# A graph network on one core: a smaller descriptor scratch, and a longer ring of gathered rows

## The chip, the core and the metric

The kernel runs on one core of one Trainium2 chip. The metric is device microseconds of one execution: the kernel before took 3387.86 us (median of 3 runs, 3387.04 to 3388.99).

## The reference, cut to what matters

A graph of 3125 nodes with 128 features and 50000 edges, sorted by destination, goes through a two-layer graph convolution (its input rows are all the same row, so it needs no gather), and then through five attention layers with two heads. The attention layers take most of the time. One of them, in the reference's words:

```python
edge_emb = edge_attr_full @ ew.T + eb
xw = x @ W
xj = xw[src].reshape(-1, H, D) + edge_emb.reshape(-1, H, D)
xi = xw[dst].reshape(-1, H, D)
alpha = einsum('ehd,hd->eh', xi, att_i) + einsum('ehd,hd->eh', xj, att_j)
alpha = leaky_relu(alpha, 0.2)
ea = exp(alpha - segment_max(alpha, dst)[dst])
alpha = ea / (segment_sum(ea, dst)[dst] + 1e-16)
out = segment_sum(xj * alpha[..., None], dst).mean(axis=1) + b
```

Each edge needs the row of its source node (`src` is random), and each node is also its own neighbour, by 3125 added self edges that carry no attributes.

## The kernel before, in words

**Tiles, groups and chunks.** The edges are cut into 391 tiles of 128. Four tiles make a group (98 groups), and 28 tiles make a chunk: chunks 0 to 12 have 28 tiles, chunk 13 has 16, chunk 14 has 11 (`CH`, `TC`, `GROUPS`, lines 45 to 51). Every layer goes once over all of them.

**The gathers.** At the start of a layer SP writes the node table (a row is 128 features and two scores) to memory in five pieces. When these have landed, POOL issues 391 indirect DMAs, one a tile: each fetches 128 rows of 520 bytes by the indices in `srci` into one slot of `ring`, a buffer of `RING` = 60 slots (lines 502 to 513). Tile t goes to slot (t + 25) % `RING` (line 68): the first 25 slots hold the nodes' own rows `xt` at the start of a layer, so the first gathers go behind them. Three waits hold a gather back:

```python
if t == RING - SHIFT:
    pool.wait_ge(aj_read, layer + 1)
if RING - SHIFT <= t < RING - SHIFT + NT:
    pool.wait_ge(tr_ps, NT * layer + t - (RING - SHIFT) + 1)
if t >= RING and (t == RING or GROUP_OF[t - RING] != GROUP_OF[t - RING - 1]):
    pool.wait_ge(sums, layer * G + GROUP_OF[t - RING] + 1)
```

The first two (from tile 35 on with 60 slots) wait until `xt` has been read by VectorE (line 1208) and transposed by TensorE (line 758). The third, from tile 60 on, waits until TensorE has summed the group that last lay in the slot. A gather raises one of five semaphores `gath`, by its chunk's number modulo five, when it has landed.

**A chunk's way through the engines.** ScalarE copies, for each tile, a window of 24 destination scores (`windows`, line 580). VectorE reduces these windows (`windows_sum`, lines 1087 to 1096). Then `chain_scan` (lines 1099 to 1123) waits until all gathers of the chunk have landed, adds the sources' scores out of `ring` (line 1105, and line 1108 in addition where the chunk's slots wrap past the end of the ring), and starts a running maximum. `chain_rows` and `chain_cols` (lines 1125 to 1156) end it, ScalarE takes the exponential (line 586), and `chain_probs` (line 1166) writes the weights and makes the first two groups' one-hot weights with `weigh` (line 1161).

**Sums.** For each group TensorE clears a bank (line 741), and for each of its tiles multiplies the ring's rows by the weights (line 745) and the edges' attributes by the one-hots (line 747); the last of them raises `sums`. VectorE adds the bank into `acc` (`add_group`, line 1200). In chunks 0 to 8 up to three tiles of a second product, `self_tile` (line 783), go between a chunk's groups.

**The order of the work** is written out by hand in each engine's program. On VectorE the chain of chunk c+1 is laid into the groups of chunk c: the windows' sums behind its first three groups, `chain_scan` behind the add of its third group, rows and columns behind the fourth, `chain_probs` behind the sixth (`chain_at`, line 89). `weigh` runs four groups ahead of `add_group`. In chunk 13 the places are the first, second and third group.

**The end of a layer.** When all groups are added, 25 node tiles are multiplied, scaled, added and written back to `xt`, and the next layer's table is written.

**The scratch.** The descriptors of the gathers are generated on the chip into a reserved stretch at the front of each partition of SBUF, by default 16 KB long (`dynamic_dma_scratch_size` of the constructor at line 1368).

Of the kernel before, what the change touches and what calls it, by code (L numbers as in the profile page):

```python
# [48 lines left out]
G = len(GROUPS)  # L49
GC = [[g for g in range(G) if GROUPS[g][0] == c] for c in range(NC)]  # L50
GROUP_OF = [g for g in range(G) for _ in range(GROUPS[g][2])]
RING = 60
SHIFT = 25
NGATH = 5
NAT = 3
# [7 lines left out]
POOL_MUL = (1, 3, 5)  # L63
assert TC[NC] == REAL and RING >= SHIFT + NT


def slot(t):
    return (t + SHIFT) % RING

# [28 lines left out]
def program(nc, x, src_rows, src_key, src_flat, dst_col, dst_next_col, dst_flat, dst_first,  # L98
            attr, W1, b1, W2, b2,
            weights, weightsT, attT, edge_w, edge_b, edge_woT, biases, edge_bias, out):  # L100
    with ExitStack() as ctx:
        def sb(name, shape, dt=F32):
            return ctx.enter_context(nc.sbuf_tensor(name, shape, dt))
# [13 lines left out]
        ai_rows = sb("ai_rows", [P, H, NP])  # L117
        ring = sb("ring", [P, RING, ROW])
        onehot = sb("onehot", [P, TILES, WIN])
# [67 lines left out]
        def part(base, n, dt=F32):  # L187
            words = n if dt != BF16 else (n + 1) // 2
            v = base[:, cut[0]:cut[0] + words]
            cut[0] += words  # L190
            return v if dt == F32 else v.bitcast(dt)[:, 0:n]
# [43 lines left out]
        s_parts = part(rowsf, 3 * NT, BF16).rearrange("p (q h) -> p q h", q=3)  # L235
        assert cut[0] <= RING * ROW
        cut[0] = NT * ROW
# [229 lines left out]
        def _(pool):  # L467
# [32 lines left out]
            for layer in range(LAYERS):  # L500
                pool.wait_ge(table_w, 16 * (len(TABLE_CUTS) - 1) * (layer + 1))
                for t in range(REAL):
# [4 lines that stand above are left out]
# [871 lines left out]
```

## Time and profile before

| what | value |
|---|---|
| time, median of 3 runs | 3387.86 us (3387.04 to 3388.99) |
| the profiled execution, first to last instruction | 3764.7 us |
| before the first gather | 475.5 us |
| a layer's gathers, first to last issue (layers 1 to 5) | 565.7, 567.9, 568.6, 566.0, 566.6 us |
| from a layer's last gather to the next layer's first (after layers 1 and 2) | 92.0, 89.1 us |
| busy: TensorE, VectorE, ScalarE, POOL | 65%, 53%, 19%, 59% |
| granted TensorE clock, mean | 0.537 |

The profile shows one execution, which is not one of the three timed ones; of its own time no more than the span is given. All parts of the time are read from this one execution, and a wait is put down to what released it: "issue" is time in which the engine waited for nothing that the profile shows, "remote" a release from outside the engines that are recorded.

### The profile page before, as it was taken

What the parts mean: (1) busy time and instruction counts of PE and PEld (TensorE: products, weight loads), DVE (VectorE), ACT (ScalarE), POOL (GpSimd) and SP (SyncE); (2) the same over time, 40 slices, a digit from 0 to 9 for tenths busy, and PEclk for the clock granted to TensorE, in tenths of its full rate; (3) what the DMA queues carried; (4) which work ended last, traced back from release to release, by engine and by line L of the source; (5) the groups of instructions that cost most, each with busy time, mean ns of one, the idle gap of its engine ahead of it and who ended that gap; (6) DMA issues with size and microseconds to landing.
All of it is one profiled execution on the core that took longest, in us unless ns stands there. A gap on an engine that the chain in (4) does not pass through costs nothing.

```text
span 3764.7 us, 48376 instructions
## 1 busy us (share of the span) xinstructions
PE 2439.0 (65%) x13595; PEld 2001.4 (53%) x13595; DVE 2004.0 (53%) x6216; ACT 696.7 (19%) x3102; POOL 2210.5 (59%) x2357
## 2 busy tenths in 40 slices
PE   6779726666582766658276665837576582766668
PEld 6679615555461655547165554725455461655546
DVE  8955624554472555547255554725454472555456
ACT  0078511111121111112111111211111121111112
POOL 0067466666626766662666666266676626666661
PEclk8555555555565555556555555655555565555556
DMA  3212122222202222221222222022222202222221
GB/s 101 97 60 80 30 52 54 53 52 57 49 24 51 54 51 53 56 49 30 47 54 52 53 56 49 25 53 54 50 53 57 50 24 50 54 50 53 52 49 40
DMA packets 114121, 195.78 MB, mean 52 GB/s; under 512 B 39897, under 2 KB 77272, under 8 KB 113864
## 3 DMA queue, kind: packets, MB, share of 16 engines
q0 software_dynamic: 62560, 130.25, 15.2%
q1 hardware_dynamic: 51304, 62.42, 5.3%
q8 instruction: 122, 2.00, 0.2%
q14 instruction: 135, 1.11, 0.1%
HBM read 180.86 MB, written 11.67 MB: 51 GB/s over the span
## 4 chain that ended last, share of the span: by engine, by line
DVE 36%; PE 25%; another core or an unknown queue 20%; issue 13%; DVEq 3%; POOL 1%; ACT 1%; ACTq 1%; DMA 0%; POOLq 0%
PE bank L745 10%; PE bank L747 6%; DVE acc L1200 4%; DVE into L1143 2%; DVEq L1016 2%; PE bank L718 2%; DVE pw L1161 2%; DVE alpha L1094 2%; PE bank L741 2%; PE bank L783 2%; DVE fwd L1150 2%; DVE lanes L1129 2%; DVE prod L1072 1%; PE bank L766 1%
## 5 line engine op out<-in xcount | busy, mean ns | idle before, releaser
L510 POOL DMA_INDIRECT ring<-table,srci x1955 | 1941.2, 993 | 937.6 <-issue 556.4
L745 PE MATMUL bank<-pw,ring 128*128 128x48 f32 x3910 | 1210.9, 404 | 203.3 <-issue 201.8
L745 PEld LDWEIGHTS bank<-pw,ring 128*128 128x128 f32 x3910 | 1014.9, 314 | 302.9 <-issue 231.1
L1200 DVE TENSOR_TENSOR acc<-acc,bank 128x288 f32 x490 | 222.8, 455 | 1128.7 <-remote 857.3
L747 PE MATMUL bank<-onehot,est 128*36 128x24 f32 x3910 | 632.6, 243 | 222.9 <-issue 221.7
L741 PE MATMUL bank<-zeros 128*128 128x288 bf16 x490 | 208.5, 426 | 697.1 <-DVE pw L1161 438.7
L747 PEld LDWEIGHTS bank<-onehot,est 128*36 128x36 f32 x3910 | 391.2, 149 | 393.9 <-issue 226.6
L741 PEld LDWEIGHTS bank<-zeros 128*128 128x128 bf16 x490 | 55.4, 113 | 752.0 <-DVE pw L1161 453.3
L586 ACT ACTIVATE dd<-dd 128x66 f32<-128x66 f32 x75 | 19.4, 258 | 2163.4 <-DVE dd L1154 1177.9
L580 ACT COPY ai_win<-ai_rows 128x48 f32 x1955 | 336.3, 229 | 432.6 <-issue 410.5
L491 POOL TENSOR_TENSOR ring<-ring,acc 128x512 f32<-128x512 f32 x98 | 117.1, 1195 | 250.1 <-ACT ring L545 246.7
L517 POOL TENSOR_TENSOR S<-S 128x128 f32<-128x128 f32 x125 | 57.4, 459 | 323.6 <-ACT S L590 319.2
L783 PE MATMUL bank<-Wl,S 128*128 128x258 f32 x250 | 152.8, 697 | 50.1 <-issue 48.7
L718 PE MATMUL bank<-onehot,ring 128*128 128x24 f32 x784 | 172.2, 388 | 18.4 <-ACT ring L556 7.9
L718 PEld LDWEIGHTS bank<-onehot,ring 128*128 128x128 f32 x784 | 169.3, 331 | 21.1 <-DVE bank L1043 8.8
L1091 DVE TENSOR_TENSOR ai_win<-ai_win,onehot 128x1344 f32<-128x1344 f32 (+2 forms) x75 | 109.1, 1455 | 122.5 <-issue 101.2
L1161 DVE TENSOR_TENSOR pw<-onehot,est 128x192 f32<-128x192 f32 x490 | 160.0, 352 | 0.1
L556 ACT ACTIVATE ring<-ring,acc 128x128 f32<-128x128 f32 x392 | 124.3, 389 | 29.4 <-PE bank L718 24.7
L1143 DVE COPY into<-carry 2x96 f32<-2x96 f32 x300 | 93.6, 312 | 45.9 <-issue 33.8
L800 PE MATMUL bank<-El,acc 128*128 128x256 f32 x250 | 95.8, 470 | 23.8 <-DVE y L1305 20.0
L1094 DVE TENSOR_REDUCE alpha<-ai_win 128x56 f32<-128x1344 f32 (+2 forms) x75 | 108.6, 1448 | 0.0
L783 PEld LDWEIGHTS bank<-Wl,S 128*128 128x128 f32 x250 | 64.6, 308 | 70.3 <-issue 63.8
(214 smaller groups left out, 2610.1 us busy)
## 6 DMA issues: line engine op xcount, KB each, us to landing
ring<-table,srci POOLq DMA_INDIRECT x1955
ai_rows<-lo_dram SPq DMA_DIRECT2D x28, 896.0 KB, 4.3
at<-in_attr SPq DMA_DIRECT2D x65, 224.0 KB
table<-ring SPq DMA_DIRECT2D x15, 390.0 KB, 3.5
table<-ring SPq DMA_DIRECT2D x5, 325.0 KB, 3.4
result<-ring SPq DMA_DIRECT2D x24, 64.0 KB
x_mid<-ring SPq DMA_DIRECT2D x3, 384.0 KB, 2.7
table<-ring SPq DMA_DIRECT2D x5, 130.0 KB, 2.4
```

What stands on the lines that cost most here:

```text
L510: nc.gpsimd.indirect_dma_start(out=ring[:, slot(t), :], out_offset=None, in_=table, in_offset=bass.IndirectOffsetOnAxis(ap=srci[:, t:t + 1 ...
L556: ins = nc.scalar.activation(rows[:, g % 3, k, :], pre[:, g % 3, k, :], ACT.Relu, scale=n_e[:, t:t + 1])
L580: ins = nc.scalar.copy(ai_win[:, t - TC[c] + k, :, :], ai_rows[:, :, bass.ds(base[k], WIN)])
L718: ins = nc.tensor.matmul(total[:, at_k], rows[:, g % 3, k, :], onehot[:, t0 + k, :], start=False, stop=k == GRP - 1, skip_group_check=True)
L741: nc.tensor.matmul(total, zeros[:, 0:P], zeros[:, :], start=True, stop=False, skip_group_check=True)
L745: nc.tensor.matmul(wide[:, 0:H, at_k], ring[:, slot(t), 0:D], pw[:, g % DEEP, k, :, :], start=False, stop=False, skip_group_check=True)
L747: ins = nc.tensor.matmul(wide[0:EC, H, at_k], est[:, c % 2, t - TC[c], :], onehot[:, t, :], start=False, stop=k == n - 1, skip_group_check ...
L783: nc.tensor.matmul(bank[3][:, 0:H * D + H], S[:, j, D:2 * D], Wl[:, layer % 2, :], start=True, stop=True).then_inc(s_ps, 1)
L1094: link(V.tensor_reduce(alpha[:, :, 0:k].rearrange("p h k -> p k h"), win, AX, ALU.add))
L1143: ins = V.tensor_copy(into[i * QB:i * QB + H, :, :], carry[:, :, 1 + i:1 + P:NQB])
L1161: V.tensor_tensor(pw[:, g % DEEP, 0:n, :, :], onehot[:, t:t + n, :].unsqueeze(2).broadcast_to((P, n, H, WIN)), est[:, c % 2, k:k + n, HF:H ...
L1200: V.tensor_tensor(win, win, grp_sum(g).rearrange("p (r w) -> p r w", r=REG), ALU.add)\
```

## The change

The module's constant `RING` goes from 60 to 83: 23 slots more of 130 words, which is 11,960 bytes of each partition. The constructor is told to reserve 4096 bytes for the gathers' descriptors where its default is 16,384, which gives 12,288 bytes back. Everything that is worked out from `RING` moves with it: a tile's slot, the tile from which the gathers wait for `xt` (35 to 58), the tile from which they wait for sums (60 to 83), and which chunks wrap around the ring's end.

```diff
-RING = 60
+RING = 83
...
-    nc = bacc.Bacc("TRN2", target_bir_lowering=False, num_devices=1)
+    nc = bacc.Bacc("TRN2", target_bir_lowering=False, num_devices=1, dynamic_dma_scratch_size=4096)
```

## Rows read from the trace of the kernel before

**Rows 1.** The page, span and busy time of each engine.

```profile
span 3764.7 us, 48376 instructions
...
PE 2439.0 (65%) x13595; PEld 2001.4 (53%) x13595; DVE 2004.0 (53%) x6216; ACT 696.7 (19%) x3102; POOL 2210.5 (59%) x2357
```

**Rows 2.** The page's groups: busy, mean ns, idle before, and its releaser.

```profile
L510 POOL DMA_INDIRECT ring<-table,srci x1955 | 1941.2, 993 | 937.6 <-issue 556.4
L745 PE MATMUL bank<-pw,ring 128*128 128x48 f32 x3910 | 1210.9, 404 | 203.3 <-issue 201.8
...
L747 PE MATMUL bank<-onehot,est 128*36 128x24 f32 x3910 | 632.6, 243 | 222.9 <-issue 221.7
...
L580 ACT COPY ai_win<-ai_rows 128x48 f32 x1955 | 336.3, 229 | 432.6 <-issue 410.5
```

**Rows 3.** One line's instructions, L1105: min/median/max ns, and its idle time's releasers.

```profile
L1105 DVE TENSOR_TENSOR alpha<-alpha,ring x75: 177/251/263, 512.6 to 3706.1; 128x56 f32<-128x56 f32 x35, 128x22 f32<-128x22 f32 x10, 128x14 f32<-128x14 f32 x5, 128x30 f32<-128x30 f32 x5
...
  DMA ring<-table,srci: 8.3, 1
```

**Rows 4.** The same view of the gathers, L510.

```profile
L510 POOL DMA_INDIRECT ring<-table,srci x1955: 942/947/2335, 475.5 to 3675.6; - x196
```

**Rows 5.** Stretches of layer 2 (length, then PE, PEld, DVE, ACT, POOL): gathers, end.

```profile
1133.20:1701.10 567.90, 335.22 (x1544) 269.79 (x1542) 266.31 (x817) 74.96 (x404) 386.10 (x391) 0.51 0.22 52
1701.10:1790.20 89.10, 75.68 (x373) 62.21 (x373) 68.96 (x287) 26.58 (x92) 21.37 (x52) 0.67 0.09 27
```

**Rows 6.** TensorE in time (start, length), a group and a self tile undisturbed.

```profile
2710.39 0.42 PE L741 MATMUL bank<-zeros 128*128 128x288 bf16 x1
...
2713.80 1.23 PE L783 MATMUL bank<-Wl,S 128*128 128x258 f32 x2
2714.82 0.45 PE L741 MATMUL bank<-zeros 128*128 128x288 bf16 x1
```

**Rows 7.** TensorE in time, within one group elsewhere (in brackets: idle before).

```profile
1440.13 0.24 PE L745 MATMUL bank<-pw,ring 128*128 128x48 f32 x1 [2.12 <-issue]
...
1442.93 0.20 PE L747 MATMUL bank<-onehot,est 128*36 128x24 f32 x1 [1.86 <-issue]
```

**Rows 8.** ScalarE in time, the window copies of layer 2's first chunk.

```profile
1150.95 1.77 ACT L580 COPY ai_win<-ai_rows 128x48 f32 x10 [2.63 <-DVE ai_rows L525]
...
1155.81 0.23 ACT L580 COPY ai_win<-ai_rows 128x48 f32 x1 [1.87 <-issue]
```

**Rows 9.** VectorE in time: layer 1, chunk 0's scan; layer 2, chunk 14.

```profile
512.64 0.26 DVE L1105 TENSOR_TENSOR alpha<-alpha,ring 128x56 f32<-128x56 f32 x1 [8.33 <-DMA ring<-table,srci]
...
1728.10 0.20 DVE L1105 TENSOR_TENSOR alpha<-alpha,ring 128x22 f32<-128x22 f32 x1
...
1738.06 0.62 DVE L1161 TENSOR_TENSOR pw<-onehot,est 128x192 f32<-128x192 f32 x2
```

**Rows 10.** POOL in time: the gather of tile 60 in each layer, and two more.

```profile
560.02 0.94 POOL L510 DMA_INDIRECT ring<-table,srci  x1 [8.38 <-remote]
...
1221.18 0.95 POOL L510 DMA_INDIRECT ring<-table,srci  x1 [12.04 <-PE bank L747]
...
1226.94 0.96 POOL L510 DMA_INDIRECT ring<-table,srci  x1 [0.30 <-issue]
...
1390.34 0.96 POOL L510 DMA_INDIRECT ring<-table,srci  x1 [0.30 <-issue]
...
1879.68 0.95 POOL L510 DMA_INDIRECT ring<-table,srci  x1 [12.77 <-PE bank L747]
...
2535.62 1.49 POOL L510 DMA_INDIRECT ring<-table,srci  x1 [7.29 <-remote]
...
3196.84 0.94 POOL L510 DMA_INDIRECT ring<-table,srci  x1 [11.76 <-PE bank L747]
```

**Rows 11.** The gathers between the two at 1226.94 and 1390.34, grouped by line.

```profile
L510 POOL DMA_INDIRECT ring<-table,srci x113 | 111.9, 990 | 51.5 <-issue 32.0 <-remote 16.5 <-PE bank L747 3.0
```

**Rows 12.** One line's instructions, L1108: min/median/max ns.

```profile
L1108 DVE TENSOR_TENSOR alpha<-alpha,ring x30: 154/198/228, 568.2 to 3615.3; 128x42 f32<-128x42 f32 x5, 128x34 f32<-128x34 f32 x5, 128x26 f32<-128x26 f32 x5, 128x18 f32<-128x18 f32 x5
```

## The prediction, made before the change was run

> **What bounds the kernel now.** I read the page first. No engine is full: the busiest, TensorE, works 65% of the span, POOL 59% [rows 1]. So the time lies in who waits for whom, and for a ring that is to be longer there are two questions: does POOL wait for a free slot, and does anybody wait for a gather?
>
> POOL does wait. A gather takes 947 ns in the median [rows 4] and the next follows 0.30 us later [rows 10], a step of 1.25 us, so 391 of them would take 489 us; in layer 2 they take 567.9 us [rows 5]. In every layer the gather of tile 60, the first that needs a used slot, stands 7.3 to 12.8 us [rows 10], and shorter waits follow later.
>
> But nobody waits for the gathers. The line that would is `chain_scan`'s first instruction, L1105. Of its 75 executions one found VectorE idle until a gather landed, the first of all, for 8.3 us [rows 3, 9]. In the other 74 the chunk was there before VectorE came to it. In this execution the loop of TensorE, VectorE and ScalarE sets the pace, and POOL, held by the ring, follows.
>
> Why is that loop slow? Undisturbed, a group takes TensorE 2713.80 - 2710.39 = 3.41 us and a self tile 1.02 us more [rows 6]; a chunk of seven groups and three self tiles is 26.9 us, against 28 x 1.25 = 35.0 us for its gathers. The measured pace is 567.9 / 391 x 28 = 40.7 us. The difference lies in slow stretches in which an engine issues one instruction per 0.7 us or a multiple of it, waiting for nothing that the profile shows. TensorE has idle times of 2.12 and 1.86 us in the middle of a group [rows 7]; ScalarE makes ten window copies in 1.77 us and then single ones with 1.87 us of nothing before them [rows 8]. Over the run such "issue" time ahead of the two matmuls of a group is 201.8 + 221.7 = 423.5 us [rows 2].
>
> This matters for carrying the trace over to the time. The span is 3764.7 us [rows 1], the median of the timed runs 3387.86 us: 376.8 us less, 75 per layer. The slow stretches are about the only thing of that size (423.5 / 5 = 85 per layer), so I take it that the timed runs have few of them. Then the loop needs some 27 to 30 us a chunk and the gathers 35, and the timed runs are paced by POOL: 391 gathers of 990 ns [rows 11] (993 over all layers [rows 2]) and 390 gaps of 0.30 are 504 us, 64 less than the 567.9 of the profile. The other 11 of the 75 would come out of the 89.1 us between two layers' gathers [rows 5], which start with a backlog in the profile. So the profile and the timed runs are bound by different things, and the change has to be priced for both.
>
> **The ring, in the profile's execution.** The wait at tile 60 goes, since a slot is needed again only at tile 83, 23 x 1.25 = 29 us later. POOL is up to 23 tiles further ahead; then it is held at the loop's pace again. Late next is what was late before: the loop. As 74 of 75 scans did not wait, rows that land earlier start nothing earlier. At a layer's end POOL is done with its gathers earlier and then waits longer for ScalarE's scaled rows. Gain 0.
>
> **The ring, in the timed runs.** Is there a wait for a slot at all, when POOL sets the pace? At a layer's start: the first scan comes with its landed gathers at 512.64 - 475.5 = 37.1 us after the first gather [rows 4, 9]. From a scan to its weights an undisturbed chain takes 1738.06 - 1728.10 = 10.0 us, with two adds in it, and 0.35 for the first of the two weights that last 0.62 together [rows 9]; that is the chunk of 11 tiles, and for 28 I add an estimated 1.3 us for its longer rows. The group takes 3.4 us. So slot 0's rows are summed at 37.1 + 11.7 + 3.4 = 52.2 us, and the gather of tile 60 comes at 60 x 1.25 = 75.0 us: 23 us to spare. Within a layer: tile 28c+60 is the 33rd gather after chunk c's last, 41.3 us later. The scan comes 37.1 - 27 x 1.25 = 3.4 us after that last issue, then 11.7 for the chain, about 2.4 for three more adds and weighs in between, and 3.4 for the group: 20.9 us, with 20 to spare. Sixty slots are enough, and 83 change nothing. If that cover is gone, that is if slow stretches of over 20 us fall between scan and sum, a wait as in the profile is there; that is the first rival.
>
> **Waits that move.** The waits for `xt` move from tile 35 to tile 58. They held no gather at 35: in layer 2 the first 60 gathers took 1221.18 - 12.04 - 1133.20 = 75.9 us, 1.27 each, with no room for a wait [rows 5, 10]. So they hold none at 58. On POOL nothing is queued behind a gather but more gathers and the end of the layer.
>
> **The split scan.** L1108 runs where a chunk wraps: 30 times now, 198 ns in the median [rows 12]. With 83 slots, chunk c starts at (28c + 25) modulo 83 (chunk 14 at 405 - 4 x 83 = 73), and chunks 2, 5, 10 and 14 wrap: 20 times. Those of chunks that are hidden cost nothing either way. Chunk 14 is new, and its scan stands on the path to the layer's end: 5 x 0.2 = 1.0 us more; bounds 0 and 5 x 0.23 = 1.1.
>
> **The scratch.** A gather that goes around the scratch's end should show. The gathers at 1226.94 and 1390.34 last 0.96 us, a hundredth over their neighbours, and 113 gathers lie from one to the other [rows 10, 11]; I take these for the turns. A quarter of the scratch then turns every 28 gathers: 1955 / 28.3 = 69 times in place of 17, 52 more. At a hundredth of a microsecond each that is 0.5 us, on the path where POOL sets the pace. The other end: a turn (or a full scratch) that waits for the landing of the gather before, 3.4 - 1.25 = 2.1 us x 52 = 109 us. I take 0.5, as the turns that the trace shows are that cheap, and keep 109 as a rival. To fill the smaller scratch 28 gathers would have to be under way; at 3.4 us from issue to scan there are not more than three.
>
> By the Trainium skill, page "DMA: Bandwidth & Descriptors" (sections "Terms" and "The descriptor swizzle"), a descriptor is 16 bytes, lies in a ring in SBUF, and a transfer over 128 partitions takes nine per engine on each side. By that, 16,384 / 16 / 9 = 113.8 gathers go around once and 28.4 in the small scratch, and the rows agree with the 113. It would speak against the change only with 29 gathers in flight.
>
> **Sum.** 0 for the ring, + 1.0 for chunk 14, + 0.5 for the turns: + 1.5 us. On the profiled execution: 3764.7 + 1.5 = 3766.2 us of span. On the median: 3387.86 + 1.5 = 3389.4, call it 3389 us. A measurement of this kernel tells about 0.2% (7 us) from no change.
>
> **Rivals.**
>
> *The wait at tile 60 is in the timed runs too, and POOL paces the rest of the layer.* Then the five waits go: 8.38 + 12.04 + 12.77 + 7.29 + 11.76 = 52.2 us [rows 10], less five ordinary gaps, 50.7 us: 3337 us; with half of the slow stretches perhaps half of it, 3362. For it: the waits are there in every layer, and slow stretches are seen right in the layers' starts [rows 8]. Against it: it needs two things that exclude each other in the profile, slow engines at the start and a slow POOL afterwards; and the margin worked out above is 23 us. Chance 0.24, spread from 3337 to 3380.
>
> *The small scratch holds gathers back.* Place: POOL, every 28th gather. Price: 109 us, 3497 us. It decides from 7 / 52 = 0.13 us a turn on. Against it: the turns of 0.96. Chance 0.05.
>
> *More gathers beside the chain.* The slow stretches shown lie inside a layer's gathers [rows 7, 8]. If gathers cause them, and some are in the timed runs, 23 gathers more run beside the first chunk's chain in each layer. By TensorE's 423.5 us over 1955 gathers, 0.22 us each: 5 x 23 x 0.22 = 25 us, 3413 us. Against it: the number of gathers is the same, and POOL is only earlier. Chance 0.05.
>
> By the Trainium skill, page "SBUF — State Buffer" (section "SBUF: two separate sides"), a gather's descriptors wait while VectorE holds the port that it shares with POOL. That would stretch gathers that move beside VectorE's long instructions, and spare those that move away from them. The longest gather here, 2335 ns beside 947 [rows 4], may show it; the mean is 993 [rows 2], 46 ns over the median, so 115 moved gathers could gain or lose 5 us by it, inside the bound of no change.
>
> **How the numbers follow.** The forecast holds 0.66, the three rivals 0.24, 0.05 and 0.05. From these: faster by over 0.2% 0.24, within it 0.66, slower 0.10. The likeliest case's own range is 3381 to 3395. The range that is to hold the time 8 times in 10 reaches into the first rival, to 3350 (a wait of some 7.5 us a layer gone), and up to 3396.
>
> **What would show it.** In the profile after, right: no long idle time at tile 60 and a first one near tile 83; L1105 again almost never idle for a gather; L1108 20 times; gathers a hundredth longer every 28; a span within a few us of 3764.7, with slow stretches as before. Wrong: gathers of 1.5 us or more at every 28th; scans that wait for gathers; or a time 20 us and more below 3387.86, which would mean that in the timed runs POOL both waits for slots and sets the pace.

## The result, and the profile after

The changed kernel takes 3513.88 us (median of 4 runs, 3513.61 to 3515.98), against 3388.0 us for the kernel before in 4 runs: a ratio of 1.0374, with a 95% interval of 1.0359 to 1.0388. It is slower by 126 us, where the prediction said 3389 and gave 0.10 to slower.

The execution whose trace stands ahead of the prediction (span 3764.7 us [rows 1]) was 377 us longer than the timed runs of the kernel before, so its slow stretches can't be typical of them. The kernel before was profiled once more (time 3385.25 us), and it is this second profile that answers to the one after. The page of the kernel before, second profile (span, busy time, then the groups as in [rows 2]):

```profile
span 3383.4 us, 48376 instructions
...
PE 2404.6 (71%) x13595; PEld 1979.6 (59%) x13595; DVE 2004.1 (59%) x6216; ACT 669.5 (20%) x3102; POOL 2227.8 (66%) x2357
...
L510 POOL DMA_INDIRECT ring<-table,srci x1955 | 1959.0, 1002 | 633.1 <-issue 569.6
L745 PE MATMUL bank<-pw,ring 128*128 128x48 f32 x3910 | 1217.3, 411 | 0.0
...
L1105 DVE TENSOR_TENSOR alpha<-alpha,ring 128x56 f32<-128x56 f32 (+7 forms) x75 | 18.0, 240 | 755.2 <-DMA ring<-table,srci 755.0
...
L580 ACT COPY ai_win<-ai_rows 128x48 f32 x1955 | 309.2, 228 | 57.8 <-issue 22.6
```

The page of the changed kernel:

```profile
span 3514.1 us, 48366 instructions
...
PE 2405.5 (68%) x13595; PEld 1980.4 (56%) x13595; DVE 2004.5 (57%) x6206; ACT 669.5 (19%) x3102; POOL 2225.9 (63%) x2357
...
L510 POOL DMA_INDIRECT ring<-table,srci x1955 | 1956.9, 1001 | 771.8 <-issue 730.6
L745 PE MATMUL bank<-pw,ring 128*128 128x48 f32 x3910 | 1216.8, 411 | 0.0
...
L1105 DVE TENSOR_TENSOR alpha<-alpha,ring 128x56 f32<-128x56 f32 (+5 forms) x75 | 18.0, 240 | 884.6 <-DMA ring<-table,srci 884.4
...
L580 ACT COPY ai_win<-ai_rows 128x48 f32 x1955 | 309.1, 228 | 57.9 <-issue 22.7
```

Three things are to be seen. The work is the same: no busy time of these groups moves by more than 2.1 us. TensorE's idle time before L745, 203.3 us in [rows 2], is 0.0 in both. And POOL's idle time before its gathers rises from 633.1 to 771.8, by 138.7 us, and VectorE's wait for the gathers from 755.2 to 884.6, by 129.4. The views of waits (total, times, longest), kernel before in its second profile and then changed, have 65 waiting scans of the 75 in both, where [rows 3] had one:

```profile
DVE alpha L1105 <- DMA ring<-table,srci: 755.0, 65, 17.0
...
DVE alpha L1105 <- DMA ring<-table,srci: 884.4, 65, 18.2
```

So VectorE waits for gathers before the change as after it, and with the change they come later.

Where do they lose the time? The stretches of [rows 5] (length, then PE, PEld, DVE, ACT, POOL; at the end the granted clock, the DMA share and GB/s), kernel before in its second profile:

```profile
1056.40:1566.70 510.30, 347.87 (x1621) 279.21 (x1619) 279.39 (x867) 69.42 (x406) 391.43 (x391) 0.51 0.25 58
1566.70:1639.40 72.70, 59.60 (x297) 48.56 (x297) 55.37 (x236) 26.32 (x91) 21.35 (x52) 0.73 0.11 32
```

and changed:

```profile
1084.81:1622.30 537.49, 347.76 (x1627) 279.48 (x1626) 280.31 (x866) 70.37 (x412) 390.91 (x391) 0.51 0.24 55
1622.30:1693.91 71.61, 58.38 (x289) 48.13 (x289) 54.65 (x236) 25.27 (x85) 21.36 (x52) 0.71 0.12 33
```

A layer's 391 gathers take 27.2 us more, and its end 1.1 us less. POOL in time shows how (start, length, in brackets the idle time before); the gathers number 27, 28, 55 and 56 of the first attention layer, counted from 0, in the changed kernel:

```profile
511.08 0.94 POOL L510 DMA_INDIRECT ring<-table,srci  x1 [0.30 <-issue]
514.38 0.95 POOL L510 DMA_INDIRECT ring<-table,srci  x1 [2.35 <-issue]
...
549.60 0.94 POOL L510 DMA_INDIRECT ring<-table,srci  x1 [0.30 <-issue]
552.96 1.00 POOL L510 DMA_INDIRECT ring<-table,srci  x1 [2.42 <-issue]
```

and the gathers that start from 514.3 to 552.9, grouped by line:

```profile
L510 POOL DMA_INDIRECT ring<-table,srci x28 | 27.9, 998 | 10.6 <-issue 10.6
```

Every 28th gather has 2.4 us of idle time before it, put down to "issue", for which the profile names no releaser. There are 13 such gaps in each layer (at gathers 28, 56 and so on to 364), and in the five layers' gathers no other gap of over 0.34 us. A gap is 2.42 us in the mean, 2.12 over the ordinary 0.305: 65 x 2.12 = 138 us, which is POOL's whole 138.7. The five layers' gathers take 537.5, 537.5, 535.4, 537.1 and 536.7 us, in the mean 27.1 more than in the second profile of before (508.5, 510.3, 509.3, 511.3, 509.3); five times that is 136, and the ends give some 5 back: 131 us, the difference of the spans, 3514.1 - 3383.4 (the medians of the timed runs are 126 apart).

In the second profile of the kernel before, the same places have nothing. Its gathers 27 and 28, and then 59 and 60, the last of them the one that had 8.38 us before it in [rows 10]:

```profile
509.75 0.94 POOL L510 DMA_INDIRECT ring<-table,srci  x1 [0.30 <-issue]
510.99 0.94 POOL L510 DMA_INDIRECT ring<-table,srci  x1 [0.30 <-issue]
...
550.64 0.94 POOL L510 DMA_INDIRECT ring<-table,srci  x1 [0.30 <-issue]
551.88 0.95 POOL L510 DMA_INDIRECT ring<-table,srci  x1 [0.30 <-issue]
```

### The profile page after: what moved, and what is told of

It is laid out like the page before. It is cut to its first block, busy times and chain, and to the rows that moved or that the text cites. A ratio compares the mean times of both kernels' runs of the same rounds, so it can differ in the third digit from the quotient of the medians.

```text
span 3514.1 us, 48366 instructions
## 1 busy us (share of the span) xinstructions
PE 2405.5 (68%) x13595; PEld 1980.4 (56%) x13595; DVE 2004.5 (57%) x6206; ACT 669.5 (19%) x3102; POOL 2225.9 (63%) x2357
## 3 DMA queue, kind: packets, MB, share of 16 engines
q14 instruction: 135, 1.11, 0.1%
## 4 chain that ended last, share of the span: by engine, by line
POOL 50%; issue 21%; DVE 15%; PE 11%; DMA 1%; ACT 1%; DVEq 1%; POOLq 0%; ACTq 0%
POOL ring L510 48%; PE bank L745 4%; PE bank L747 2%; PE bank L718 2%; DVE prod L1072 2%; DVE ring L847 1%; POOL ring L491 1%; DVE ai_rows L940 1%; PE bank L741 1%; DVE y L1299 1%; DVE y L1305 1%; DMA ring<-table,srci 1%; DVE acc L944 1%; DVE prod L1269 1%; DVE acc L1200 1%
## 5 line engine op out<-in xcount | busy, mean ns | idle before, releaser
L510 POOL DMA_INDIRECT ring<-table,srci x1955 | 1956.9, 1001 | 771.8 <-issue 730.6
L745 PE MATMUL bank<-pw,ring 128*128 128x48 f32 x3910 | 1216.8, 411 | 0.0
L745 PEld LDWEIGHTS bank<-pw,ring 128*128 128x128 f32 x3910 | 1009.1, 316 | 103.7 <-issue 23.9
L747 PE MATMUL bank<-onehot,est 128*36 128x24 f32 x3910 | 619.1, 246 | 0.0
L1105 DVE TENSOR_TENSOR alpha<-alpha,ring 128x56 f32<-128x56 f32 (+5 forms) x75 | 18.0, 240 | 884.6 <-DMA ring<-table,srci 884.4
L747 PEld LDWEIGHTS bank<-onehot,est 128*36 128x36 f32 x3910 | 382.5, 150 | 177.6
L580 ACT COPY ai_win<-ai_rows 128x48 f32 x1955 | 309.1, 228 | 57.9 <-issue 22.7
L556 ACT ACTIVATE ring<-ring,acc 128x128 f32<-128x128 f32 x392 | 124.3, 389 | 29.3 <-PE bank L718 24.7
```

Source lines behind the costliest of these rows:

```text
L510: nc.gpsimd.indirect_dma_start(out=ring[:, slot(t), :], out_offset=None, in_=table, in_offset=bass.IndirectOffsetOnAxis(ap=srci[:, t:t + 1 ...
L556: ins = nc.scalar.activation(rows[:, g % 3, k, :], pre[:, g % 3, k, :], ACT.Relu, scale=n_e[:, t:t + 1])
L580: ins = nc.scalar.copy(ai_win[:, t - TC[c] + k, :, :], ai_rows[:, :, bass.ds(base[k], WIN)])
L745: nc.tensor.matmul(wide[:, 0:H, at_k], ring[:, slot(t), 0:D], pw[:, g % DEEP, k, :, :], start=False, stop=False, skip_group_check=True)
L747: ins = nc.tensor.matmul(wide[0:EC, H, at_k], est[:, c % 2, t - TC[c], :], onehot[:, t, :], start=False, stop=k == n - 1, skip_group_check ...
```

## The experiments

The theory: the small scratch has room for 28 gathers, and when it is full POOL waits until a gather has landed. The rivals: the longer ring (or where it puts the rows) costs the time; or each turn of a scratch costs it, full or not. All edits are against the kernel before. Where no ratio is given, the kernel ran once.

**Each half of the change alone, and two other scratches.** The ring stays at 60 slots, and the scratch is 4, 8 or 2 KB; then 16 KB with 50 slots used of a buffer of 60.

```diff
-    nc = bacc.Bacc("TRN2", target_bir_lowering=False, num_devices=1)
+    nc = bacc.Bacc("TRN2", target_bir_lowering=False, num_devices=1, dynamic_dma_scratch_size=4096)
```

> The small scratch alone: 4096 bytes, ring back at 60. Theory T (the scratch is full after 28 gathers, and POOL then waits until the gather before has landed, 2.1 us over an ordinary gap): as slow as the change, 3514 us, with a gap of about 2.4 us at every 28th gather, 13 in a layer, and 884 us in which VectorE waits for gathers. Rival R (the 23 gathers more that run ahead of the sums are what costs): the scratch alone costs nothing, 3388 us, and no gap at every 28th gather.

Measured: 3514.09 us, ratio 1.0367 (1.0350 to 1.0384). The same 13 gaps a layer stand at the same gathers, and POOL's "issue" time in the view of waits (total, times, longest) is

```profile
POOL ring L510 <- issue: 712.8, 1902, 2.5
```

So the scratch alone is the whole loss.

```diff
-RING = 60
+RING = 50
+ROOM = 60
...
-        ring = sb("ring", [P, RING, ROW])
+        ring = sb("ring", [P, ROOM, ROW])
...
-        assert cut[0] <= RING * ROW
+        assert cut[0] <= ROOM * ROW
```

> The full scratch of 16384 bytes, and of the 60 slots 50 are used, so that the ring is shorter by 10 where the change made it longer by 23. Theory T: the ring was never what held the timed runs (52 us from a layer's first gather to the first sum, 62.5 us to the gather of tile 50; 21 us against 28.8 later in the layer), so 3388 us, within 0.2%, with no gaps at every 28th gather. Rival R (how far the gathers run ahead matters): a change of time the other way round, some 20 to 60 us off 3388. A third view, that 60 slots were just short in the timed runs: slower, by 8 us a layer or more, 3430 us.

Measured: 3386.77 us, ratio 0.9991 (0.9982 to 1.0001), no gap over 0.34 us. Ten slots fewer hold nothing, as the prediction's margin of 23 us at tile 60 has it (at tile 50 it would be 23 - 10 x 1.25 = 10).

```diff
-    nc = bacc.Bacc("TRN2", target_bir_lowering=False, num_devices=1)
+    nc = bacc.Bacc("TRN2", target_bir_lowering=False, num_devices=1, dynamic_dma_scratch_size=8192)
```

> Half the default scratch, 8192 bytes, ring 60. Theory T with a price for each time around: the scratch is full every 56 gathers, 6 times in a layer, 30 in all, 30 x 2.1 = 64 us: 3450 us, gaps of 2.4 us at every 56th gather. Rival F (a full scratch costs nothing as long as what is to be freed lies far enough behind; at 4096 bytes alone it does not): 3388 us and no gaps.

Measured: 3390.67 us, ratio 1.0001 (0.9992 to 1.0011), no gaps:

```profile
POOL ring L510 <- issue: 569.0, 1867, 0.3
```

A scratch of 8 KB turns 34 times, twice as often as the 16 KB of before, and costs nothing. The rival of a price for each turn is out.

```diff
-    nc = bacc.Bacc("TRN2", target_bir_lowering=False, num_devices=1)
+    nc = bacc.Bacc("TRN2", target_bir_lowering=False, num_devices=1, dynamic_dma_scratch_size=2048)
```

> An eighth of the default scratch, 2048 bytes, ring 60. Theory T: full every 14 gathers, 27 times in a layer, 135 in all; 135 x 2.1 = 286 us: 3674 us, gaps at every 14th gather. If the wait were tied to something else that comes every 28 gathers (a chunk has 28 tiles), the gaps would stay at every 28th and the time at 3514 us.

Measured: 3641.18 us, ratio 1.0742 (1.0725 to 1.0760). The gaps stand at every 14th gather, 27 in a layer, here gathers 13 and 14 of the first:

```profile
492.28 1.18 POOL L510 DMA_INDIRECT ring<-table,srci  x1 [0.31 <-issue]
495.73 0.95 POOL L510 DMA_INDIRECT ring<-table,srci  x1 [2.27 <-issue]
```

With some 2.28 us each, 135 x (2.28 - 0.305) = 267 us. The gathers themselves were 3 us longer in all and the layers' ends 3.3 us shorter each, so the span grew by 3637.5 - 3383.4 = 254. Half the scratch has twice the gaps, of nearly the same length (seven of the 135 have 2.8 to 3.2 us). The gaps move with the scratch, so the start of a chunk, which has 28 tiles too, isn't what makes them.

**Does the longer ring give anything where the scratch costs nothing?** 8 KB leave room for 76 slots.

```diff
-RING = 60
+RING = 76
...
-    nc = bacc.Bacc("TRN2", target_bir_lowering=False, num_devices=1)
+    nc = bacc.Bacc("TRN2", target_bir_lowering=False, num_devices=1, dynamic_dma_scratch_size=8192)
```

> The longer ring without the wait: 8192 bytes of scratch, and 76 slots, as many as fit beside it. Theory T (the scratch alone made the change slow, and the ring never held the timed runs): 3388 to 3390 us, no difference. Rival: a longer ring lets POOL run on where 60 held it: 20 to 50 us faster, 3340 to 3370 us.

Measured: 3388.01 us, ratio 1.0001 (0.9991 to 1.0010), no gaps. The longer ring gives nothing. Beside it ran the kernel before, without an edit, for a second profile:

> The kernel before, unchanged, for a second profile. If the profile that the prediction was read from was of an execution with slow stretches that the timed runs don't have: a span within 5 us of the time, 3385 us, no gap over 0.4 us between two gathers of a layer, tile 60 included, and VectorE idle for gathers in most of the 75 scans, some 750 us. If the slow stretches belong to the kernel under the profiler: a span near 3765 us again.

Measured: 3385.25 us; its rows stand in the section above. No gather waits for a slot.

**How much scratch is enough?** First a little more than 4 KB.

```diff
-    nc = bacc.Bacc("TRN2", target_bir_lowering=False, num_devices=1)
+    nc = bacc.Bacc("TRN2", target_bir_lowering=False, num_devices=1, dynamic_dma_scratch_size=4608)
```

> A scratch of 4608 bytes, which by the turns of 14 at 2048 and 28 at 4096 has room for 31 gathers; ring 60. Theory M (what POOL can free when the scratch is full goes up to a mark, and marks stand every so many gathers, more than 28 and at most 56; without a mark behind it, it waits for the newest): with marks every 32, as now, a gap of 2.4 us at every 31st gather, 12 in a layer, some 3500 us. Theory S (each time around costs the wait, only 8192 bytes are over a limit of size): the same. If marks stand at 28 or 30: no gaps, 3388 us.

> 5120 bytes, room for 35 gathers; ring 60. Theory M with marks every 32: when the scratch is full the mark lies three gathers behind, 3.75 us, and has landed (3.4 us): no gaps, 3388 us, within 5 us. Theory S, or marks farther apart than 35: gaps of 2.4 us at every 35th gather, 11 in a layer, 55 x 2.1 = 115 us: 3500 us.

Measured: 3389.39 us with 4608 bytes and 3386.71 us with 5120 (same line, other number), no gaps in either. So a full scratch isn't dear in itself: with 4608 bytes, an eighth more, every gap is gone. "Full, then wait for the newest gather" would have kept them at a longer distance, and so would the expected marks at every 32nd gather. Something between 4096 and 4608 bytes decides. Three sizes between, one in each run:

```diff
-    nc = bacc.Bacc("TRN2", target_bir_lowering=False, num_devices=1)
+    nc = bacc.Bacc("TRN2", target_bir_lowering=False, num_devices=1, dynamic_dma_scratch_size=4160)
...
+    nc = bacc.Bacc("TRN2", target_bir_lowering=False, num_devices=1, dynamic_dma_scratch_size=4224)
...
+    nc = bacc.Bacc("TRN2", target_bir_lowering=False, num_devices=1, dynamic_dma_scratch_size=4352)
```

> 4160 bytes: more than 4096, but by the turns of 14 at 2048 and 28 at 4096 still room for 28 gathers (4160 / 4096 x 28.4 = 28.9). Theory M29 (POOL can free a full scratch only up to a mark, and a mark comes with the 29th gather): as at 4096, gaps of 2.4 us at every 28th gather, 13 in a layer, 3508 us of span. Theory L (a limit of size: what is over 4096 bytes has no wait): no gaps, 3385 us.

> 4224 bytes, room for 29 gathers. Theory M29: the mark is the newest gather, which POOL must wait for: gaps of 2.4 us at every 29th gather, 13 in a layer, 3505 us. A mark with the 28th gather: it lies one gather behind, gaps of 2.4 - 1.25 = 1.1 us, 3430 us. Theory L: no gaps, 3385 us.

> 4352 bytes, room for 30 gathers. Theory M29: the mark lies one gather behind, gaps of 2.4 - 1.25 = 1.1 us at every 30th gather, 13 in a layer: 65 x 0.85 = 55 us, 3440 us. A mark with the 28th gather: two behind, no gap. Theory L: no gaps, 3385 us.

Measured: 3512.93, 3440.04 and 3389.75 us, with 3388.88 for the kernel before beside them. At 4160 bytes all is as at 4096, gaps of 2.4 us at every 28th gather. At 4224 there is a step between: gathers 27, 28 and 29 in time,

```profile
509.90 0.94 POOL L510 DMA_INDIRECT ring<-table,srci  x1 [0.30 <-issue]
511.15 0.94 POOL L510 DMA_INDIRECT ring<-table,srci  x1 [0.30 <-issue]
513.23 0.95 POOL L510 DMA_INDIRECT ring<-table,srci  x1 [1.13 <-issue]
```

the gathers up to then, grouped by line (the idle time is that before the layer's first),

```profile
L510 POOL DMA_INDIRECT ring<-table,srci x29 | 27.8, 958 | 30.8 <-DMA table<-ring 22.3 <-issue 8.5
```

and POOL's waits:

```profile
POOL ring L510 <- issue: 647.5, 1942, 1.3
```

One more gather fits, 29, so the first gap stands at gather 29. Yet the next ones stand at 57, 85 and 113: still every 28th. That is near what was expected of a mark with the 28th gather (1.1 us, 3430 us). And it isn't the newest gather that is waited for: number 29 goes out 513.23 - 511.15 = 2.08 us after number 28, but 513.23 - 509.90 = 3.33 after number 27; in the changed kernel number 28 goes out 514.38 - 511.08 = 3.30 us after number 27. In both the wait ends when some 3.3 us have passed since gather 27.

That is later than the rows of gather 27 have landed. The first scan waits for gathers 0 to 27, and in the changed kernel it starts 0.74 us before gather 28 does:

```profile
513.64 0.26 DVE L1105 TENSOR_TENSOR alpha<-alpha,ring 128x56 f32<-128x56 f32 x1 [18.21 <-DMA ring<-table,srci]
```

The DMA packets in the traces show what the wait follows. In the changed kernel the last packet of gather 27 ends at 513.24, and over all 65 gaps POOL goes on 1.11 to 1.19 us after the last packet of the gather before. With 4224 bytes it goes on 1.11 to 1.18 us after the last packet of the gather before that one, while the newest is just landing. In the seven long gaps with 2048 bytes the gather before landed late, 2.8 to 3.3 us after its issue where 2.2 is usual. So the wait follows the landing of one certain gather, and not a fixed time.

At 4352 bytes, gathers 27 to 30:

```profile
509.90 0.94 POOL L510 DMA_INDIRECT ring<-table,srci  x1 [0.30 <-issue]
511.15 0.95 POOL L510 DMA_INDIRECT ring<-table,srci  x1 [0.30 <-issue]
512.40 0.94 POOL L510 DMA_INDIRECT ring<-table,srci  x1 [0.30 <-issue]
513.65 0.95 POOL L510 DMA_INDIRECT ring<-table,srci  x1 [0.30 <-issue]
```

Number 29, which waited with 4224 bytes, doesn't wait here, so there is room for 30 at least, and number 30 is the first that could have to wait. It is due 3.75 us after number 27, and the 3.3 are over. No gap.

**The change with 384 bytes more.** If this is all, the change with a slightly larger scratch loses nothing.

```diff
-RING = 60
+RING = 83
...
-    nc = bacc.Bacc("TRN2", target_bir_lowering=False, num_devices=1)
+    nc = bacc.Bacc("TRN2", target_bir_lowering=False, num_devices=1, dynamic_dma_scratch_size=4480)
```

> The change as it is, with 83 slots, but 384 bytes more of scratch: 4480 bytes, room for 31 gathers. Theory M28 (POOL frees a full scratch up to a mark that comes with every 28th gather and waits until that gather has landed; three gathers behind, 3.75 us, it has): no gaps, and all of the change's loss is gone: 3388 us, within 0.2%. Rival: part of the loss belongs to 83 slots together with a small scratch: between 3395 and 3514 us.

Measured: 3384.46 us, ratio 0.9992 (0.9982 to 1.0002), on its page

```profile
span 3381.7 us, 48366 instructions
...
L510 POOL DMA_INDIRECT ring<-table,srci x1955 | 1959.3, 1002 | 633.9 <-issue 587.8
```

and in its view of waits

```profile
POOL ring L510 <- issue: 587.8, 1929, 0.3
```

No wait of POOL's for a gather's issue is over 0.3 us. The 126 us are gone with the ring of 83 still there. The 384 bytes are the only difference to the changed kernel, so the cause is the size of the scratch, and all of the loss comes and goes in a narrow step, between 4160 and 4352 bytes. No version beats the kernel before by more than can be measured.

## Why the prediction was wrong

**What bounds the kernel: right.** The prediction read out of a profile that was 377 us longer than the timed runs that those have few slow stretches and are paced by POOL. The second profile shows it: 755.0 us of VectorE's time go into waiting for gathers, and the layers' gathers take 508 to 511 us against 504 worked out (the gathers' mean was 1002 ns, not 990). One of the prediction's signs of being wrong, "scans that wait for gathers", could therefore decide nothing: 65 of 75 waited before the change already.

**The ring: right.** Sixty slots hold no gather in the timed runs (tile 60 follows after 0.30 us), fifty hold none either, and 76 or 83 gain nothing. The first rival, 3337 to 3380 us, is out with that. The third is out too: TensorE's idle time before L745 is 0.0 before and after, and ScalarE's "issue" time before L580 22.6 and 22.7 us. For an execution with slow stretches the step stays untested, as the profile after was not of that kind.

**The split scan: not visible.** L1108 runs 20 times, as worked out (before: x30 [rows 12]):

```profile
L1108 DVE TENSOR_TENSOR alpha<-alpha,ring x20: 153/202/252, 591.3 to 3455.6; 128x2 f32<-128x2 f32 x10, 128x52 f32<-128x52 f32 x5, 128x54 f32<-128x54 f32 x5
```

The 1.0 us that chunk 14's part of it was to cost is below what these runs can tell.

**The scratch: wrong, and this is the step that failed.** The prediction took 0.5 us "as the turns that the trace shows are that cheap", and dismissed the wait because "to fill the smaller scratch 28 gathers would have to be under way". Both sentences rest on the same unspoken assumption: that a gather's room is free again as soon as it has landed. The term of 0.5 us was 138 us of POOL's time in the trace and 126 us in the timed runs. The count of gathers under way was right: no gather is issued with more than two others still landing in the changed kernel. What was wrong is the assumption, and the gaps show it. In the changed kernel gather 28 was due at 511.08 + 0.94 + 0.30 = 512.3 us. Of the 28 gathers before it, numbers 0 to 25 had been issued 3.7 us or more before that (number 25 two steps of 1.25 us ahead of 27's 511.08), longer than the 3.3 us after which number 27's wait ended, and still POOL stood. The DMA packets say more: the last one of gather 26 ends at 511.97, so at 512.3 number 27 alone had not landed. So gathers that had landed kept their room. What the trace of before showed, a cheap turn after 113 gathers, was a scratch that had got its room back in time; it could say nothing of one whose room is as short as what is freed at once. The turn was measured, the full scratch wasn't.

By the Trainium skill, page "DMA: Bandwidth & Descriptors" (sections "Terms" and "The descriptor swizzle"), a descriptor is 16 bytes, and a transfer of 1 MiB to 128 partitions has nine per engine on each side. Taken over to a gather of 128 rows this is an estimate of 144 bytes, by which 2048, 4096 and 4224 bytes hold 14.2, 28.4 and 29.3 gathers; the traces agree with it: first gaps at gathers 14, 28 and 29. The prediction's "only with 29 gathers in flight" was its own addition, and the measurement decides against it.

**The size, had the rival been chosen.** The second rival named the place and the mechanism and gave 3497 us, with a chance of 0.05. Its price for one wait, 2.1 us, met the 2.12 measured, but by luck. It took 3.4 us from a gather's issue to its scan, which came of setting the first 27 steps at 1.25 us each; some of those gathers lasted longer, and in the profile of [rows 9] number 27 was issued here:

```profile
510.00 0.94 POOL L510 DMA_INDIRECT ring<-table,srci  x1 [0.30 <-issue]
```

So the scan came 512.64 - 510.00 = 2.64 us after it, and the price should have been 2.64 - 1.25 = 1.4 us. What made it 2.12 all the same is that POOL goes on 0.74 us after the scan does. The rival's count was off: it took the 52 turns that are added. But the turns of before never waited, so none is to be taken off: it is 13 gaps in each layer (391 / 28 = 13.96), 65 in all, as the count begins anew with each layer, whose first gather finds everything landed. 65 x 2.12 = 138 against 52 x 2.1 = 109. The chance was the worse error: the one row that spoke against it, a turn of 0.96 us [rows 10], was of a scratch whose room had come back in time. The forecast of slower held 0.10 in all, and the range ended at 3396.

**What stays open.** Why POOL can take room back only up to certain gathers. With 4224 bytes these marks are gathers 27, 55 and so on, and the runs with 4096, 4160 and 4352 bytes fit the same row. The marks begin anew with each layer: counted on through 391 = 13 x 28 + 27 gathers, they would move by one gather from layer to layer, and they don't. What sets them isn't shown. 28 gathers are what 4096 bytes hold, but they are also a chunk, whose gathers raise one semaphore, and no run has chunks of another length. With 2048 bytes either the marks lie closer, at every 14th, or POOL waits for the newest gather where no mark lies behind. Whether the marks would lie elsewhere for gathers of another size wasn't tried.

## What to carry to other kernels

A buffer that is turned over cheaply when it is large says nothing of the time at which its room comes free; before it is made smaller, ask what returns the room, not only how much is in use. Where POOL's gathers set the pace, look at the profile for gaps of equal length at equal distance that are put down to "issue": their distance can be that of a hidden buffer that is full, which a run with another size of it tells, and the loss is about their number times what they have over an ordinary gap. A few per cent of that buffer can decide the whole of it (4160 to 4352 bytes here), so run two or three sizes around the one that is wanted.

## What the runs showed of the hardware

- A gather of 128 rows takes between 4160 / 29 = 143.4 and 4224 / 29 = 145.7 bytes of each partition's scratch, as 28 and no more fit into 4160 bytes, and 29 into 4224, if the first gap marks a full scratch.
- A gather's last DMA packet ends 2.2 us after its issue (median in the changed kernel), and the scan that waits for it starts 2.6 us after it (first scan of the first attention layer).
- With a small scratch that is full, POOL waits until some 3.3 us after the issue of one of the last gathers, which is 1.1 to 1.2 us after that gather's last packet, without any trace of it but idle time: 2.4 us at every 28th gather with 4096 and 4160 bytes (+124 to +126 us), 1.2 us with 4224 (+51), none from 4352 up to 16384. With 2048 bytes it is 2.3 us at every 14th (+251), and the wait ends 0.9 to 1.4 us after the last packet.
- For this kernel 4352 bytes of scratch do as well as the default of 16 KB, and 4224 don't: from 4352 to 8192 bytes all times lie between 3384 and 3391 us.
